# Attention with mixture-of-experts kernel: the square roots, the first heads' loads and the place of the routing are changed

## The reference

```python
xn = (x - mean) / sqrt(var + 1e-5)
p = xn @ Wv.T + bv                       # q = k = v = p, 16 heads of 8
s = softmax(q @ k.T / sqrt(8)) @ v       # per batch and head
s = s @ Wo.T + bo
z = (xn - mean) * rsqrt(var + 1e-5) * ln_g + ln_b
probs = softmax(z @ rW + rb)             # two best of 8 experts, weights w
mixed = sum over e of w[e] * (gelu(z @ W1[e] + b1[e]) @ W2[e] + b2[e])
out = x + s * silu(xn + mixed)
```

## Time and profile before

| | |
|---|---|
| median of 3 runs | 629.43 us |
| the profiled execution | 632.46 us |
| its span, first to last instruction | 630.7 us |
| TensorE busy / granted clock, mean | 571.2 us (91%) / 0.936 |
| ScalarE busy | 543.2 us (86%) |
| VectorE, GpSimd busy | 240.1 us, 230.1 us |
| 512 exponentials (line 776) | 488.9 us, 1049 ns each |

### The profile page before, as it was taken

The page is one execution under the profiler, slowest core; times in us unless marked ns, Lnnn a source line. Parts: engine busy times, 40 slices in busy tenths (PEclk is TensorE's granted clock), DMA queues, the critical chain, the costliest instruction groups (busy, mean ns, idle before and its releaser), DMA issues.

```text
span 630.7 us, 11527 instructions
## 1 busy us (share of the span) xinstructions
PE 571.2 (91%) x3990; PEld 232.3 (37%) x3990; DVE 240.1 (38%) x695; ACT 543.2 (86%) x591; POOL 230.1 (36%) x252
## 2 busy tenths in 40 slices
PE   3778884799999999799999999999988999999996
PEld 2553320223344344333444344434334343433221
DVE  5553863573333333113222232223232852223381
ACT  4576663699999999979999999999999999999994
POOL 2364047827777774254211121112203334341000
PEclk9977776799999999869999999999995999999999
DMA  6137697746466655227363445453233654442220
GB/s 164 45 101 219 231 304 276 184 132 149 110 162 133 162 96 116 70 67 160 68 153 99 127 112 132 103 135 108 70 117 108 173 167 139 130 116 83 65 66 19
DMA packets 100989, 81.54 MB, mean 129 GB/s; under 512 B 54219, under 2 KB 92638, under 8 KB 100318
## 3 DMA queue, kind: packets, MB, share of 16 engines
q1 hardware_dynamic: 94270, 71.26, 43.2%
q0 software_dynamic: 6656, 9.48, 4.8%
HBM read 58.07 MB, written 28.39 MB: 137 GB/s over the span
## 4 chain that ended last, share of the span: by engine, by line
PE 74%; ACT 9%; DVE 7%; issue 5%; DMA 4%; SPq 1%; ACTq 0%; DVEq 0%
PE bank_v L1330 35%; PE pair L1276 16%; PE bank_f L1370 8%; PE bank_f L1379 8%; ACT exps L776 7%; DMA p_dram<-w_ring 3%; PE bank_f L1347 2%; PE pair L1236 1%; ACT pre L752 1%; PE bank_f L1343 1%; PE pair L1227 1%; DMA x_tok<-in_L_attn_x 1%; DVE o_turned L1082 1%; PE bank_f L1354 1%; DVE v_tok L863 1%
## 5 line engine op out<-in xcount | busy, mean ns | idle before, releaser
L776 ACT ACTIVATE exps<-pair 128x1024 f32<-128x1024 f32 x512 | 488.9, 1049 | 54.6 <-PE pair L1276 36.3
L1330 PE MATMUL bank_v<-exps,v_tok 128*32 128x512 f32 x2048 | 285.0, 630 | 3.1 <-ACT exps L776 1.6
L687 POOL DMA_INDIRECT o_dram<-o_ring,slot_place x80 | 77.4, 968 | 238.3 <-DVE o_ring L1133 238.0
L1276 PE MATMUL pair<-q_ring,k_ring 26*128 26x512 f32 x1024 | 152.9, 513 | 2.7 <-ACT exps L776 2.1
L1276 PEld LDWEIGHTS pair<-q_ring,k_ring 26*128 26x128 f32 x1024 | 60.7, 188 | 93.4 <-ACT exps L776 54.8
L672 POOL DMA_INDIRECT z_dram<-pre,dest_i x64 | 64.3, 1004 | 52.2 <-DVE place_i L1037 33.3
L1379 PEld LDWEIGHTS bank_f<-w_ring,pre 128*128 128x128 f32 x320 | 46.2, 208 | 72.2 <-issue 43.3
L1124 DVE TENSOR_TENSOR pre<-bank_f,w_ring 128x256 f32<-128x256 f32 x80 | 33.9, 423 | 102.1 <-PE bank_f L1370 102.1
L1379 PE MATMUL bank_f<-w_ring,pre 128*128 128x128 f32 x320 | 62.5, 322 | 9.7 <-ACT pre L752 5.3
L1133 DVE TENSOR_TENSOR o_ring<-bank_f,w_ring 128x128 f32<-128x128 f32 x80 | 23.2, 290 | 124.3 <-PE bank_f L1379 121.1
L679 POOL DMA_INDIRECT place_dram<-token_place,place_i x64 | 61.3, 958 | 19.5 <-issue 19.5
(11 more groups left out here) (154 smaller groups left out, 287.1 us busy)
## 6 DMA issues: line engine op xcount, KB each, us to landing
w_ring<-w_dram SPq DMA_DIRECT2D x80, 192.0 KB
w_ring<-w_dram SPq DMA_DIRECT2D x80, 129.0 KB
q_ring<-p_dram SPq DMA_DIRECT2D x56, 104.0 KB
k_ring<-p_dram SPq DMA_DIRECT2D x56, 96.0 KB
z_dram<-s_tok SPq DMA_DIRECT2D x4, 1280.0 KB, 13.1
z_ring<-z_dram SPq DMA_DIRECT2D x80, 64.0 KB
rows_in_sb<-o_dram SPq DMA_DIRECT2D x16, 256.0 KB, 2.9
p_dram<-z_ring SPq DMA_DIRECT2D x8, 256.0 KB, 2.9
```

Of the source, the lines that this page charges most:

```text
L687: pool.indirect_dma_start(o_dram[:, :], bass.IndirectOffsetOnAxis(slot_place[:, h, 4 * k + i:4 * k + i + 1].bitcast(U32), 0), o_ring[:, q ...
L776: nc.scalar.activation(exps[:, g % ES, 2 * half:2 * half + 2, :], pair[(2 * g + half) % 3][:, :, :], ACT.Exp, scale=SCALE).then_inc(exp_do ...
L1276: ins = nc.tensor.matmul(pair[h % 3][:, j % 2, :], k_ring[32 * j:32 * j + KROWS, n % 2, kt * P:(kt + 1) * P], q_ring[32 * j:32 * j + KROWS ...
L1330: ins = nc.tensor.matmul(bank_v[32 * j:32 * j + 32, :], v_tok[:, (n // HG) * KT + kt, first:first + 32], exps[:, g % ES, j, :], start=(kt ...
```

## The change

1. The inverse roots: ScalarE takes the square root, VectorE its reciprocal and one Newton step (`invert`). A table with Sqrt is loaded first, that with Exp after the prologue. The statistics are no longer put between the steps of the roots. The root for the second norm is taken in the prologue, the rest of `norm2` stands behind the branch.
2. The third chunk of x is loaded ahead of the small inputs. The second filler of TensorE is gone.
3. The high parts of the first two blocks are stored to all their three places (4 stores a block), so units 0 and 1 are loaded in 8 transfers each; keys are loaded before the wait for the norm rows. `load_unit(1)`, the loads of rb, W1, bo and `zero_z(0)` follow the last stores, ahead of the branch. Line 586 copies the later batches alone, at place 14 of SP's order.
4. The routing, the biases (4 uses of 4 columns for 8 of 2), the norms, the scaling of W1, `zero_z(1)`, `keep_w2` (place 38 instead of 33), the first loads of W1's experts (35 and 37 instead of 29 and 31), and the experts' products move in the loop.

```diff
@@ -64,7 +63,7 @@
-WARM = (4, 4)
+WARM = 4
...
@@ -85,22 +84,23 @@
-RANK_AT = ((2, 3, 3, 4, 4, 5), (17, 18, 19, 20, 22, 23))
-COUNT_AT = (7, 24)
-ASSIGN_AT = ((7, 8, 8, 9, 10), (25, 26, 27, 28, 30))
-SCALE_Z_AT = ((5, 6, 7, 8), (18, 20, 22, 23))
-EXP_AT = (10, 21)
-WEIGH_AT = ((12, 13, 14), (31, 32, 33))
-BIAS_AT = 4
-BIAS_COLS = 2
-NORM_AT = 12
-ZERO_AT = 12
-SCALE_W1_AT = (13, 14, 15, 16)
-SCATTER_AT = (11, 31)
-MOE_AT = 37
+RANK_AT = ((6, 6, 7, 7, 8, 8), (17, 18, 19, 20, 22, 23))
+COUNT_AT = (11, 24)
+ASSIGN_AT = ((11, 12, 12, 13, 14), (25, 26, 27, 28, 30))
+SCALE_Z_AT = ((9, 10, 10, 11), (18, 20, 22, 23))
+EXP_AT = (14, 21)
+WEIGH_AT = ((15, 15, 16), (31, 32, 33))
+BIAS_AT = 22
+COPY_HI_AT = 14
+BIAS_COLS = 4
+NORM_AT = 27
+ZERO_AT = 8
+SCALE_W1_AT = (27, 28, 29, 30)
+SCATTER_AT = (15, 36)
+MOE_AT = 41
-PLACE_AT = (54, 77)
+PLACE_AT = (59, 82)
...
@@ -146,7 +146,7 @@
-        place(("norm", g), NORM_AT + g - EARLY)
+        place(("norm", g), NORM_AT + (g - EARLY) * 3 // 2)
...
@@ -401,6 +407,7 @@
+            load_x(2)
...
@@ -441,30 +448,51 @@
+            def load_keys(n):
+                for j in range(4):
+                    sp.dma_start(k_ring[32 * j:32 * j + PROWS, n % 2, :].bitcast(F32),
+                                 p_dram[(n % HG) * 4 + j, 0:PROWS, (n // HG) * S:(n // HG + 1) * S]).then_inc(kq_in[n % 2], 16)
+            def load_queries(n):
+                for j in range(4):
+                    sp.dma_start(q_ring[32 * j:32 * j + KROWS, n % 2, :].bitcast(F32),
+                                 p_dram[(n % HG) * 4 + j, HI_ROW:HEAD_ROWS, (n // HG) * S:(n // HG + 1) * S]).then_inc(kq_in[n % 2], 16)
+            def load_unit(n):
+                if n >= 2:
+                    sp.wait_ge(pv_done, (n - 1) * US)
+                if n == HG:
+                    sp.wait_ge(hi_copied, 32)
+                    for i in range(2):
+                        sp.wait_ge(m_kept[1 + i], (NB - EARLY) // 2 * 16)
+                load_keys(n)
+                load_queries(n)
-                for part in range(PARTS):
-                    row = (HI_ROW, LO_ROW)[part]
-                    sp.dma_start(p_dram[:, row:row + DK, tokens], (p_hi, p_lo)[part][:, g % 2, :]).then_inc(parts_stored[g % 2], 16)
+                hi_rows = (0, HI_ROW, LO_ROW + DK) if g < EARLY else (HI_ROW,)
+                for row in hi_rows:
+                    sp.dma_start(p_dram[:, row:row + DK, tokens], p_hi[:, g % 2, :]).then_inc(parts_stored[g % 2], 16)
+                sp.dma_start(p_dram[:, LO_ROW:LO_ROW + DK, tokens], p_lo[:, g % 2, :]).then_inc(parts_stored[g % 2], 16)
-                    for i in range(2):
-                        sp.wait_ge(parts_stored[i], 16 * PARTS)
+                    for e in range(EARLY):
+                        sp.wait_ge(parts_stored[e], stored(e))
+                    sp.wait_ge(ring_cleared, 1)
+                    load_keys(0)
-                    sp.wait_ge(ring_cleared, 1)
-                    for j in range(4):
-                        load_head(0, 0, j, 0, kq_in[0])
-                        load_stabiliser(0, j, kq_in[0])
-                if g == 3:
-                    sp.dma_start(w1_stage, W1.rearrange("e h f -> h e f")).then_inc(w1_staged, 16)
-                    sp.dma_start(rb_bc[:, :], rb.rearrange("(a d) -> a d", a=1).broadcast_to([P, E])).then_inc(bias_in, 16)
-                    sp.dma_start(bo_bc[:, :], bo.rearrange("(a d) -> a d", a=1).broadcast_to([P, D])).then_inc(bias_in, 16)
+                    load_queries(0)
+            load_unit(1)
+            sp.dma_start(rb_bc[:, :], rb.rearrange("(a d) -> a d", a=1).broadcast_to([P, E])).then_inc(bias_in, 16)
+            sp.dma_start(w1_stage, W1.rearrange("e h f -> h e f")).then_inc(w1_staged, 16)
+            sp.dma_start(bo_bc[:, :], bo.rearrange("(a d) -> a d", a=1).broadcast_to([P, D])).then_inc(bias_in, 16)
+            zero_z(0)
-                sp.wait_ge(parts_stored[i], NB // 2 * 16 * PARTS)
+                sp.wait_ge(parts_stored[i], stored(NB - 2 + i))
...
@@ -575,15 +585,13 @@
-            zero_z(0)
-            load_unit(1)
-                if g == 2:
+                if g == COPY_HI_AT:
-                        sp.dma_start(p_dram[:, row:row + DK, :], p_dram[:, HI_ROW:HI_ROW + DK, :]).then_inc(hi_copied, 16)
+                        sp.dma_start(p_dram[:, row:row + DK, EARLY * BLK:], p_dram[:, HI_ROW:HI_ROW + DK, EARLY * BLK:]).then_inc(hi_copied, 16)
...
@@ -606,7 +614,7 @@
-                    if g == (AT["up", q - 2, 3] + 1 if q >= 2 else MOE_AT - 8 + 2 * q):
+                    if g == (AT["up", q - 2, 3] + 1 if q >= 2 else MOE_AT - 6 + 2 * q):
...
@@ -703,7 +711,7 @@
-            nc.scalar.activation(act_dummy[:, :], ident[0:1, 0:1], ACT.Exp).then_inc(act_dummy_ready, 1)
+            nc.scalar.activation(act_dummy[:, :], ident[0:1, 0:1], ACT.Sqrt).then_inc(act_dummy_ready, 1)
...
@@ -716,6 +724,15 @@
+            def root(c):
+                act.wait_ge(variance_ready, c + 1)
+                if c < len(NORMS):
+                    some = slice(NORMS[c][0], NORMS[c][0] + NORMS[c][1])
+                    nc.scalar.activation(rstd[:, some], veps[:, some], ACT.Sqrt).then_inc(root_ready, 1)
+                else:
+                    nc.scalar.activation(rstd2[:, :], veps2, ACT.Sqrt).then_inc(root_ready, 1)
...
@@ -736,14 +753,21 @@
+            root(0)
+                if s == 0:
+                    root(1)
+                if 1 <= s < 3:
+                    root(s + 1)
+            act.wait_ge(act_dummy_ready, 1)
+            nc.scalar.activation(act_dummy[:, :], ident[0:1, 0:1], ACT.Exp).then_inc(act_dummy_ready, 1)
...
@@ -794,23 +818,19 @@
-            def inverse_root(variance, scale, beside=None):
+            def invert(root, variance):
-                link(nc.vector.tensor_scalar(scale.bitcast(I32), variance.bitcast(I32), 1, None, ALU.logical_shift_right), beside)
-                link(nc.vector.tensor_scalar(scale.bitcast(I32), scale.bitcast(I32), -1, RSQRT_SEED, ALU.mult, ALU.add), beside)
-                for _ in range(NEWTON):
-                    link(nc.vector.scalar_tensor_tensor(out=some, in0=scale, scalar=-0.5, in1=scale, op0=ALU.mult, op1=ALU.mult), beside)
-                    link(nc.vector.tensor_tensor(some, some, variance, ALU.mult), beside)
-                    link(nc.vector.scalar_tensor_tensor(out=scale, in0=some, scalar=1.5, in1=scale, op0=ALU.add, op1=ALU.mult), beside)
+                link(nc.vector.reciprocal(root, root))
+                link(nc.vector.scalar_tensor_tensor(out=some, in0=root, scalar=-0.5, in1=root, op0=ALU.mult, op1=ALU.mult))
+                link(nc.vector.tensor_tensor(some, some, variance, ALU.mult))
+                link(nc.vector.scalar_tensor_tensor(out=root, in0=some, scalar=1.5, in1=root, op0=ALU.add, op1=ALU.mult))
-                t = next(tiles, None)
-                if t is None:
-                    return None
+                t = next(tiles)
...
@@ -822,17 +842,23 @@
-                link(nc.vector.tensor_scalar(veps[:, some], mv[:, some, 1], EPS, None, ALU.add), beside)
-                inverse_root(veps[:, some], rstd[:, some], beside)
+                nc.vector.tensor_scalar(veps[:, some], mv[:, some, 1], EPS, None, ALU.add).then_inc(variance_ready, 1)
+                if beside is not None:
+                    beside()
+                dve.wait_ge(root_ready, c + 1)
+                invert(rstd[:, some], veps[:, some])
+            def variance2():
+                nc.vector.scalar_tensor_tensor(out=veps2, in0=veps[:, :], scalar=EPS, in1=mv[:, :, 1],
+                                               op0=ALU.mult, op1=ALU.add).then_inc(variance_ready, 1)
-                link(nc.vector.scalar_tensor_tensor(out=veps2, in0=veps[:, :], scalar=EPS, in1=mv[:, :, 1],
-                                                    op0=ALU.mult, op1=ALU.add))
-                inverse_root(veps2, rstd2[:, :])
+                dve.wait_ge(root_ready, len(NORMS) + 1)
+                invert(rstd2[:, :], veps2)
...
@@ -886,24 +912,21 @@
-            def beside_norm(c):
-                if c == 0 and links[0] == 7:
-                    keep_m2()
-                else:
-                    statistics()
-            for t in range(7):
-                statistics()
-            link(statistics())
+            def take(count):
+                for _ in range(count):
+                    ins = statistics()
+                link(ins)
+            take(8)
-            norm1(0, *NORMS[0], lambda: beside_norm(0))
+            norm1(0, *NORMS[0], keep_m2)
-            norm1(1, *NORMS[1], statistics)
-            assert statistics() is None
-            keep_p(0)
+            take(8)
+            norm1(1, *NORMS[1])
+            take(16)
-            for g in range(1, NB):
+            variance2()
+            for g in range(NB):
...
@@ -911,8 +934,6 @@
-                elif g == 4:
-                    norm2()
...
@@ -1164,6 +1185,7 @@
+            norm2()
...
@@ -1195,7 +1217,7 @@
```

(39 more changed lines are left out.)

15 lines of the change are left out of this document (8 added, 7 removed).

## The result

The changed kernel takes **639.18 us** (638.05 to 640.80, 4 runs), that before 630.12 us (628.19 to 631.27, 4 runs): a ratio of 1.0149, 95% interval 1.0113 to 1.0184. It is slower by 1.5%; the forecast was 622.5 us with a range of 606 to 635. The profiled execution took 640.8 us, with a span of 639.1 us against 630.7.

A forecast was written before the change was run, and what follows sets the result against it. The loss was put at the front: 52.7 us of prologue and about 31 of stalls. The terms put the first product at 153.2 instead of 160.2 us; the 7.0 gained, off the 629.43 median, gave 622.5 us, range 606 to 635.

The forecast's parts named there:

- the rest of steps 22 to 41: Beyond 35.0 us of bare steps: biases 3.0, norms 0.6, turn and projection 0.7, VectorE overload 0.7, norm store 3.5, clock restarts 1.5.
- the bo stall: Before step 11: bo lands at 60.4, so VectorE's routing delays the output's turn; a new stall of some 12 us.
- steps 11 to 22: VectorE's work before the next output turn sets step 18 at 88.6 us; from 73.2, step 22 comes at 96.2.
- SP late 12: Before the first expert product at step 41: z's loads stand behind SP's W1 and W2 issues; 12 us taken, 9 to 16 kept.
- The bound of 5 us more: Bound on the stall before step 11: 5 us more if bo lands behind the unit's loads.
- the doubt of 3 us: Steps 11 to 22: at 1.84 us a step, step 22 would come at 93.4 instead of 96.2, so 3 us in doubt.
- Behind it ... the same: After the first expert product: number of products, gelus and tail unchanged, so nothing gained or lost there.
- The prologue: Before the first exponential: it starts at 40.3 us, 12.4 us earlier, with 2 us left on each side.
- A: Rival, the queue keeps up: bo lands sooner, the norm store costs nothing, SP late by 9 or less; 613 us, chance 0.25.
- B: Rival, the copies ahead: z's loads land behind W2, a 16 us stall; 626.5 us, or 628.5 with the clock, chance 0.17.
- C: Rival, z behind a flood: z takes 12.7 us to land, a 26 us stall before the first product; 636.5 us, chance 0.18.
- D: Rival in the prologue: Sqrt's table lacks what ScalarE needs, two loads per root, about 10 us; 632 us, chance 0.02.

The follow-up runs named there:

- w2_early: The changed kernel with SP's copies of W2 and b2 and the clearing of places at place 14 instead of 38; 628.41 us, ratio 0.9966 to the kernel before.
- bo_early: The changed kernel with the loads of rb and bo issued ahead of SP's loop over the blocks; 627.29 us, ratio 0.9954 to the kernel before.
- both_unit_later: The changed kernel with the edits of `w2_early` and `bo_early`, and unit 13 loaded three steps later; 612.12 us, ratio 0.9693 to the kernel before.
- newton_only: The changed kernel with the inverse roots as before, all on VectorE, without Sqrt; 648.59 us, ratio 1.0294 to the kernel before.
- norms_first: The changed kernel with norms 4 and 5 stored ahead of the 1 MB of scaled W1; 638.59 us, ratio 1.0148 to the kernel before.
- both_early: The changed kernel with the edits of `w2_early` and `bo_early` together; 616.07 us, ratio 0.9767 to the kernel before.
- all_mended: The changed kernel with the edits of `w2_early`, `bo_early` and `norms_first`, and unit 13 loaded later; 608.54 us, ratio 0.9646 to the kernel before.

## Why the prediction was wrong

The mechanisms of the waits held, their sizes did not; one wait, far behind, was not foreseen. The balance closes: the prediction had the first product 11.8 us too early and lost nothing behind it, where 3.6 were lost; that is 15.4, the whole difference of 639.1 and 623.7. The steps that failed are five terms of the sum, all too small: the lateness of SP by 3.2 us, the rest of steps 22 to 41 by 3.5, the bo stall by 3.2, steps 11 to 22 by 1.9, and what stands behind the first product by 3.6. No single one turns the gain of 7.0 us into the loss of 8.4; the full price of SP alone would have given 626.5.

1. **"SP late 12" was the largest miss that I chose.** The prediction worked out 16.0 from rows and took 12, "since the transfers around are fewer than at 118 us". TensorE waited 15.19 us (ScalarE 15.95). The issues from the first W1 load to the first of z took 20.3 us (20.1 predicted), at the undiminished price: the eight of b2 took 7.85 where 7.56 was the row and 4.8 the hope. TensorE asked 13.2 us after step 34 (149.8, 136.6), as predicted. The row measured the thing itself, and the ground for the discount was wrong: in the stretch of these issues the DMA share is 0.60 before and after, at 163 and 171 GB/s (118.28 to 138.39, 139.31 to 159.64). `w2_early` shows the mechanism: with ten of these copies issued elsewhere the wait is 2.37 us.
2. **The rest of steps 22 to 41**: norm wait 6.0, predicted 3.5 (+2.5). The norm row went out behind the scaled W1 at 127.18, and VectorE could read for it at 134.52, so its landing took up to 7.3 us, where 4.9 to 6.9 were allowed. Four steps, three with a bias use and one with a count, took some 2.42 us each (103.59 to 113.25), 0.57 over the bare 1.84, where 0.75 was predicted for a bias; all else together is +1.0. The 1.5 us for restarts at the lower clock had no row, and no run measures them apart.
3. **The bo stall.** Mechanism and place right: step 11 at 76.43, predicted 73.2. bo went out at 56.94 (54.8) and landed in 7.9 us, not 5.6: +4.4, of which the shorter routing gave 1.2 back. The bound of 5 us more held it. `bo_early` shows the cause: without bo's lateness the wait of 12.76 us is not there.
4. **Steps 11 to 22** took 24.9 us for 23.0: one more wait for VectorE's turn, 2.16 us at 95.39, within the doubt of 3 us that I named.
5. **"Behind it ... the same" failed** by 3.6 us. I moved the products' steps and did not walk SP's order past them: unit 13's 8 loads now stand ahead of two loads of rows. `both_unit_later` shows it.

The prologue was right within its 2 us: 41.73 for 40.3, first split at 21.43 (21.9), end of the last query issue at 38.2 (37.4), the Exp load hidden at 38.99. Its sum has a gap: 37.4 and a landing of 2.2 us make 39.6, and the 0.7 us up to 40.3 have no name; the run shows 3.5 us from that issue's end to the exponential. Its reasons were thinner too: I valued the roots by the first group's chain, but in the changed order, where `keep_p(0)` stands behind the third norm, `newton_only` shows them to be worth 5.6 us, 3.2 of them through the third group on VectorE. That the total came out close is in part luck. What the early chunk of x and the missing filler did was not tried.

**The rivals.** A (the queue keeps up) is refuted: bo and the norm row took longer to land than the main case had them (7.9 for 5.6, up to 7.3 for at most 6.9), and SP was late by 15.2 us, not by 9 or less. B gave 16 us, the right size, by another cause: z was not behind W2's copies in landing, it was issued behind them. The four loads that the first product needs went out from 159.64 to about 162.1 (4 of 12 in 7.29 us), and the turn started at 164.20, some 2.1 us later. The landing was short; the wait was SP's order. The rule of the Trainium skill, "DMA: Bandwidth & Descriptors", section "Queues, rings and completion order", that a completion count lands only after the engine's earlier writes, is neither shown nor refuted by z. The norm row fits it: issued behind 1 MB of scaled W1, it held TensorE for 4.70 us, and with the order turned (`norms_first`) the wait was gone; but transfers that merely share the engines would do the same, and no run tells the two apart. C (z lands in a flood) is refuted by the same 2.1 us: slower came, without its mechanism. What happened is no rival but the dear ends of the main case taken together: SP at 16 (+4), bo 5 us later, the norm at 5 (+1.5) and the doubt of 3 us read 622.5 + 13.5 = 636.0, and no rival held them. They were treated as if independent, although SP's one queue stands behind three of the four. D is refuted: the prologue has one load of each table, at 0.80 and 38.99, and none between the roots.

**What the change cost as a whole.** It moved work out of a stretch with stalls into one that had none, and with it SP's copies of W2 from a time when SP ran ahead to one when it was on the path.

## What to carry over

Walk each in-order queue as a schedule of its own. For every transfer that a consumer needs, list all that is issued ahead of it since the last wait, and put bulk copies that nobody awaits where the queue is idle, even if they take three times as long there (30.0 us for 10.8 in `w2_early`). Where a row measures the very sequence, take its price without a discount. If several terms hang on one cause, move them together. A stall that vanishes from the front can uncover the next one (bo, then W1; norm, then z): re-read the trace after each mend before the gain is claimed.

## What the hardware showed

**VectorE and GpSimd in step.** Instructions of 128x16 that take 0.17 us alone took 0.52 to 1.13 us beside GpSimd's, each ending 0.03 us after one of them, 3.0 us over four links. The Trainium skill, "SBUF — State Buffer", section "SBUF: two separate sides", describes an exclusive lock on a port pair that both engines share: whichever instruction starts first keeps it to its end, and the other blocks. It applies this to VectorE instructions with two SBUF inputs, or in a two-port mode. Three of the four links have two inputs; the trace doesn't show whether the first (23.22, one input) ran in such a mode. The rows agree with the lock, but no run takes GpSimd away to show it. Between them one link of 0.17 us (25.93) slipped through. Here, with GpSimd beside the chain, leaving links out was worth more than their count says.

**The price of an issue.** SP's time for the same ten copies was 10.8 us after the change and 30.0 us (22.21 + 7.81) in `w2_early`, where they stand behind 5 MB of zeros and the high rows. The DMA share was 0.64 in the first case (147.6 to 158.5 us, 195 GB/s) and 0.87 in the second (62 to 94 us, 323 GB/s). So the same copies can cost their queue three times as much; what held the issues no run shows.

**The clock.** In `w2_early` the granted clock was 0.50, the level of 1.2 GHz, from 110 to 121 us, with TensorE busy 11.00 of 11 us and its longest idle time just before 0.67 us; after the change the same steps (108.4 to 116.3 us) ran at 0.79, although TensorE had been idle for the same 0.67 us just before them. `both_early` and `both_unit_later` have the same two waits of some 2.46 us, `all_mended` none. What decides it I have not found.
